# Expert weights of the last mixture loaded two units ahead into four buffers, and the next head's source terms spread one tile earlier

## What is computed

```python
scores = x @ router_w.T + router_b                  # x = layernorm of the running rows, 625 x 768
w, ids = two largest of softmax(scores), normalised # 2 of 8 experts for each row
y_e    = x @ expert_w[e].T + expert_b[e]            # expert_w[e]: 768 x 768, float32
out    = sum over the two chosen e of w_e * y_e
```

## Time and profile before

| | |
|---|---|
| median of 3 runs | 3059.64 us (3055.92 to 3059.67) |
| the profiled execution | 3062.38 us |
| its span, first to last instruction | 3060.6 us |
| busy: PE, DVE, ACT, POOL | 2528.6, 2157.8, 1362.9, 759.1 us |
| chain that ended last | PE 59%, DVE 19%, DMA 7%, POOL 6%, issue 5%, ACT 4% |
| moved by DMA | 351.82 MB, 115 GB/s in the mean |
| mean granted TensorE clock | 0.905 of full speed |
| pass 2 of the attention | about 2070 to 2180 us |
| passes 5 and 6 | about 2600 to 2665 and 2717 to 2780 us |
| units of the last mixture | about 2844 to 3028 us |

### The profile page before, as it was taken

How to read it: one execution, slowest core, us unless ns; L and a number is a source line. 1 busy time by engine, 2 the same in 40 slices (tenths; PEclk the granted TensorE clock), 3 DMA queues, 4 the chain that set the end, 5 groups by cost and what they waited for, 6 DMA issues and landing times.

```text
span 3060.6 us, 41464 instructions
## 1 busy us (share of the span) xinstructions
PE 2528.6 (83%) x12635; PEld 2024.1 (66%) x12636; DVE 2157.8 (71%) x4356; ACT 1362.9 (45%) x2651; POOL 759.1 (25%) x939
## 2 busy tenths in 40 slices
PE   5979999876999955689999999777987798888574
PEld 2536666575699934678999999736744454766573
DVE  7988888886576646788878788657764336675454
ACT  0026666562377721566656566407411100633452
POOL 4858888800066622000000000100000000001002
PEclk8979999987999985899999999888998899987797
DMA  9701100062033411777656666520000201001786
GB/s 316 246 23 34 34 31 30 21 169 84 21 45 55 40 22 35 252 254 253 226 186 218 227 224 228 172 115 1 30 31 17 67 0 47 17 1 47 269 302 210
DMA packets 83611, 351.82 MB, mean 115 GB/s; under 512 B 26984, under 2 KB 27421, under 8 KB 75950
## 3 DMA queue, kind: packets, MB, share of 16 engines
q1 hardware_dynamic: 56772, 300.70, 30.9%
q0 software_dynamic: 26656, 48.90, 5.0%
HBM read 292.28 MB, written 57.23 MB: 114 GB/s over the span
## 4 chain that ended last, share of the span: by engine, by line
PE 59%; DVE 19%; DMA 7%; POOL 6%; issue 5%; ACT 4%; SPq 0%; POOLq 0%; ACTq 0%; DVEq 0%
PE PS L853 14%; PE PS L943 10%; PE PS L990 7%; PE PS L1087 6%; PE PS L1089 3%; DMA C<-in_L_ffn_expert_w 3%; POOL logits L731 2%; PE PS L976 2%; PE PS L1106 2%; PE PS L1108 2%; PE PS L1107 2%; DVE w1s L2226 1%; DVE w3s L2319 1%; PE PS L1177 1%; DVE w2s L2231 1%
## 5 line engine op out<-in xcount | busy, mean ns | idle before, releaser
L853 PE MATMUL PS<-large_rows,turned 125*128 x1448 | 528.1, 367 | 39.5 <-issue 18.3
L853 PE MATMUL PS<-small_rows,turned 125*128 x1448 | 492.1, 343 | 0.0
L731 POOL DMA_INDIRECT logits<-lgr,key x362 | 361.8, 1000 | 248.4 <-DVE lgr L1833 175.7
L943 PE MATMUL PS<-WB,XT 128*125 128x384 f32 (+1 forms) x1120 | 389.6, 508 | 0.0
L1087 PE MATMUL PS<-urowsT,w1s 128*128 128x384 f32 (+2 forms) x1164 | 356.3, 371 | 31.5 <-DVE F L2239 19.8
L853 PEld LDWEIGHTS PS<-large_rows,turned 125*128 125x128 f32 x1448 | 272.7, 188 | 89.0 <-issue 76.7
L943 PEld LDWEIGHTS PS<-WB,XT 128*125 128x125 f32 x1120 | 213.1, 193 | 160.9 <-issue 36.3
L990 PE MATMUL PS<-F,PT 125*125 125x96 f32 (+3 forms) x1500 | 288.1, 344 | 19.2 <-ACT PT L1415 8.2
L1089 PE MATMUL PS<-urowsT,w1s 128*128 128x192 f32 (+2 forms) x1164 | 298.6, 257 | 0.0
L853 PEld LDWEIGHTS PS<-small_rows,turned 125*128 125x128 f32 x1448 | 272.3, 188 | 8.1
L990 PEld LDWEIGHTS PS<-F,PT 125*125 125x125 f32 x1500 | 226.7, 199 | 60.9 <-issue 17.9
(11 more groups left out here) (367 smaller groups left out, 5210.9 us busy)
## 6 DMA issues: line engine op xcount, KB each, us to landing
XN<-in_L_ffn_w SPq DMA_DIRECT2D x98, 769.0 KB, 4.4
PB<-in_L_ffn_w SPq DMA_DIRECT2D x97, 768.0 KB, 5.6
WB<-node_ids SPq DMA_DIRECT2D x44, 512.0 KB
C<-in_L_ffn_expert_w SPq DMA_DIRECT2D x17, 1152.0 KB, 5.4
NEG<-in_L_ffn_expert_w SPq DMA_DIRECT2D x17, 1152.0 KB, 5.4
logits<-NEG SPq DMA_DIRECT2D x8, 1367.2 KB
WB<-logits SPq DMA_DIRECT2D x5, 2187.5 KB
slot_rows<-NEG POOLq DMA_DIRECT2D x13, 768.0 KB, 56.5
```

What stands on the lines that cost most here:

```text
L731: pool.indirect_dma_start(out=table, out_offset=bass.IndirectOffsetOnAxis(ap=key[:, i:i + 1], axis=0), in_=lgr[:, i % EU, 0:HEADS[g]["h"]] ...
L853: mm = pe.matmul(out, ohT[i % 3][:, (1 - side) * P:(2 - side) * P], part[side][:, bass.ds(c, 1), a:b].rearrange("p o n -> p (o n)"), start ...
L943: mm = pe.matmul(PS[0:R, 4 + g % 4, 0:hw], XT[:, k, t * R:(t + 1) * R], w[:, k, half * hw:(half + 1) * hw], start=(k == 0), stop=(k == kc ...
```

## The change

In the last mixture the raw weights get four buffers: C, NEG, the first 2304 columns of the transposed rows XT, and of the rows XN. Unit u uses the pair u % 2. SP loads weights(1) right behind rows(0), without waiting for a split, and in the loop rows(u + 1) and then weights(u + 2); a half of unit u + 2 waits for the split of the same half of unit u. The second pair's completion semaphores are the two that counted the logit tiles earlier (they stand at 96 then). In the attention passes of kind "gat" PE's broadcast of the next head moves from in front of the turn of tile T - 2 to that of tile T - 3.

```diff
-        uw3 = [C[...][:, 0:G3], NEG[...][:, 0:G3]]
+        uw3 = [C[...][:, 0:G3], NEG[...][:, 0:G3],
+               XTz[:, 0:G3], XN[:, :, :].rearrange("p t d -> p (t d)")[:, 0:G3]]
...
-        s_m3w = [sem(f"square_expert_weights{u}") for u in range(2)]
+        s_m3w = [sem(f"square_expert_weights{u}") for u in range(2)] + s_lt
...
                 for half in range(2):
-                    wait(sp, s_l3, 2 * u + half - 1)
-                    sp.dma_start(uw3[half], ins["L3_ffn_expert_w"][bass.ds(expert, 1)]
-                                 ...[:, half * G3:(half + 1) * G3]).then_inc(s_m3w[half], 16)
+                    wait(sp, s_l3, 2 * u + half - 3)
+                    sp.dma_start(uw3[2 * (u % 2) + half], ins["L3_ffn_expert_w"][bass.ds(expert, 1)]
+                                 ...[:, half * G3:(half + 1) * G3]).then_inc(s_m3w[2 * (u % 2) + half], 16)
...
             square_rows(0)
+            square_weights(1)
             for u in range(NS):
                 if u + 1 < NS:
                     square_rows(u + 1)
-                    square_weights(u + 1)
+                if u + 2 < NS:
+                    square_weights(u + 2)
...
                 for s in range(units):
-                    if kind == "gat" and place(s)[1] == T - 2 and place(s)[0] + 1 < h:
+                    if kind == "gat" and place(s)[1] == T - 3 and place(s)[0] + 1 < h:
                         broadcast(place(s)[0] + 1)
...
-                    act.wait_ge(s_m3w[half], 16 * (u + 1))
-                    act.copy(w3s[:, 2 * (u % 2) + half, 0, :], uw3[half]).then_inc(s_h3, 1)
+                    act.wait_ge(s_m3w[2 * (u % 2) + half], 96 * (u % 2) + 16 * (u // 2 + 1))
+                    act.copy(w3s[:, 2 * (u % 2) + half, 0, :], uw3[2 * (u % 2) + half]).then_inc(s_h3, 1)
...
-                        dve.tensor_tensor(w3s[:, 2 * (u % 2) + half, 1, :], uw3[half],
+                        dve.tensor_tensor(w3s[:, 2 * (u % 2) + half, 1, :], uw3[2 * (u % 2) + half],
```

More of the change, by code:

```diff
@@ L286, in build @@
         uexp3, uexpf3, iota3 = idx[:, 0:NS], idf[:, 0, 0:NS], idf[:, 1, 0:2 * (NU + 1)]
-        uw3 = [C[:, :, :].rearrange("p t n -> p (t n)")[:, 0:G3], NEG[:, :, :].rearrange("p t n -> p (t n)")[:, 0:G3]]
+        uw3 = [C[:, :, :].rearrange("p t n -> p (t n)")[:, 0:G3], NEG[:, :, :].rearrange("p t n -> p (t n)")[:, 0:G3],
+               XTz[:, 0:G3], XN[:, :, :].rearrange("p t d -> p (t d)")[:, 0:G3]]
         bit_q = [WB[0:R, 1536 + HB * t:1536 + HB * (t + 1)].bitcast(BF16) for t in range(T)]
@@ L376, in build @@
         s_alt = [sem(f"second_edge_logits_scattered{k}") for k in range(SLOTS)]
-        s_lt = [sem(f"logit_tile_loaded{u}") for u in range(2)]
+        s_lt = [sem(f"logit_tile_loaded_then_square_weights{u}") for u in range(2)]
         s_att = sem("attention_terms_ready")
@@ L669, in square_weights @@
                 for half in range(2):
-                    wait(sp, s_l3, 2 * u + half - 1)
-                    sp.dma_start(uw3[half], ins["L3_ffn_expert_w"][bass.ds(expert, 1)]
-                                 .rearrange("o p n -> p (o n)")[:, half * G3:(half + 1) * G3]).then_inc(s_m3w[half], 16)
+                    wait(sp, s_l3, 2 * u + half - 3)
+                    sp.dma_start(uw3[2 * (u % 2) + half], ins["L3_ffn_expert_w"][bass.ds(expert, 1)]
+                                 .rearrange("o p n -> p (o n)")[:, half * G3:(half + 1) * G3]).then_inc(s_m3w[2 * (u % 2) + half], 16)
             sp.wait_ge(s_plan, 4)
```

## The result

The changed kernel took **2979.63 us** (median of 4 runs, 2978.00 to 2981.74) beside 3059.65 us before: a ratio of 0.9738, 95% interval 0.9721 to 0.9755, or 80 us less. 3000.0 were forecast with a range from 2984 to 3019, so the sign was right and the gain was larger than the range allows. The profiled execution took 2978.18 us with a span of 2976.4, 84.2 us under the span before; 4.2 us of that is where the two profiled executions stand to their medians.

What follows compares the result with a forecast made beforehand. The last mixture was taken as bound by its load, round and split latency, the attention passes by waits around the broadcast. 3062.4 - 35 - 24.7 = 3002.7, set to 3000.0 us for the runs' lower median; range 2984 to 3019.

Steps and rivals of the forecast that it cites:

- Part 1, the loop: Last mixture: latency loop of 10.38 us a unit; four weight buffers make it DMA-bound at 8.4, gain 35 us.
- I take 375: Last mixture: assumed DMA rate in GB/s with full engines, between 363 and 396, giving 8.4 us a unit.
- the prediction's own 49.5 MB: Last mixture: what DMA moves until the last weight half has landed, 132 us at 375 GB/s.
- a PE bound of 7.6 us: Last mixture: PE's time a unit, two halves of 3.37 us and 0.82 for the turning; gain 48 us at most.
- What was called untouched: Behind the last half's landing: round, split, rest of the rows, 36 products of 8.12 us and gather stay the same.
- Part 2, pass 2: Attention pass 2: broadcast one tile earlier takes 2.1 us off ACT's wait at 7 head changes, 14.7 us.
- Passes 5 and 6: Attention passes 5 and 6: the earlier broadcast removes PE's 1.67 us of idling 6 times, 10.0 us.
- Full engines move no more than the steady row says: Mixture rival: 363 GB/s or less, gain 21 to 30 us, time 3005 to 3014; chance 0.22.
- The broadcast pays half: Attention rival: ACT's own pace or DVE also holds, part 2 gives some 12 us, time 3013; chance 0.10.
- The deeper loading isn't deeper: Mixture rival: waits for rows in SP's order hold the weights back, only part 2 counts, 3035 us; chance 0.03.
- DMA nearly as fast as PE: Mixture rival: 396 GB/s and the clock's 3 us as well, time 2990; chance 0.12.
- The slow rival's chain of row loads: Mixture rival: each row load waits for the one before, 15.1 us a unit, kernel slower at 3110; chance 0.03.

Runs made afterwards that it cites:

- the runs without the depth: The changed kernel with its four buffers, but each half of the weights loaded no earlier than in the kernel before: 3024.83 us, ratio 0.9901.

## Why the prediction was wrong

- **Part 1, the loop.** That latency bound the mixture, that loading further ahead removes it, and that DMA binds next with PE close behind: right, shown by the runs without the depth, with 24 products and with fewer stores. Issues of the same buffer were expected 16.8 us apart and were 15.07, the DMA share 1.01, row landings 7.4 (about 8 was said), half landings 10 (12 was said).
- **The term that failed is the rate.** "I take 375" came from dividing the rate by the share: 305 / 0.84 = 363 and 384 / 0.97 = 396. With full queues it was 422. At 422 GB/s the prediction's own 49.5 MB take 117.3 us and not 132, so 35 us become 49.7. The last half landed 46.8 us earlier (counted from rows(0)), where 34.9 were forecast; with 1.6 us behind it that makes the 48.4 measured. The 2.9 us between 49.7 and 46.8 are a slower beginning than reckoned: from 2808.9 to 2931.4 us the mean was 408 GB/s. The highest rate that I allowed, 396, and a PE bound of 7.6 us closed the range from below. That bound added the timeline's durations, which overlap: in the earlier trace rows the products behind a turning start 0.57 us after it and not 0.82. A unit took 6.91 us where PE bound it.
- **Why the division misleads.** The share isn't a measure of how much more could be moved: at 298, 361 and 422 GB/s it was 0.80, 0.97 and 1.01. From three to four halves the rate grew by 17% and the share by 4%. The packets for one MB took 43 us of engine time with two and with three halves outstanding and 38 with four (share times 16 engines times the stretch, by the MB moved in it). So a share of 0.97 left more room than its 3%, and a full share is no fixed rate either: from 4 to 40 us the kernel before shows 1.02 at 350 GB/s, with other transfers. Why packets get shorter when more is queued isn't shown.
- By the rule of the Trainium skill (DMA: Bandwidth & Descriptors, Where 436 GB/s comes from) that some 358 GB/s bind a core's transfers with HBM a unit would have taken 8.8 us, an estimate from its figure. The runs show 422 GB/s and 7.5 us on a core whose neighbour is idle, near the 425 that the same place names as measured; the page's note above it (Measured) says that this was a single core with the other one idle.
- **What was called untouched** gave 1.6 us: the last unit's 36 products took 6.56 us and not 8.12, at a granted clock of 1.00 and not 0.79.
- **Part 2, pass 2:** 14.7 forecast, 15.2 measured, of which ACT's wait gave 14.1. What remains of the wait is 0.9 us a change (6.1 / 7), 0.8 was reckoned.
- **Passes 5 and 6:** 10.0 forecast, 13.9 measured. The idling went as worked out (5.3 a pass with hand-overs, 5.0 forecast); the 1.6 us of each pass at the lower clock, which I had put into the upper bound alone, went too, in every trace with the broadcast at T - 3. And the products of the router's stage gained 3.1 us by the clock, which I hadn't seen at all.
- The sum of the forecast's terms at their measured sizes: 48.4 + 15.2 + 13.9 + 2.8 = 80.3 us, against 80.0 between the medians; that they agree so closely is in part luck, for the router's stage alone varies by 4 us between traces. Of the 20 us that the forecast fell short, 13.4 are the mixture's (11.9 up to the last landing, by the rate, and 1.6 behind it, by the clock), 7.2 the clock's and small change in the other stages.
- **The rivals.** "Full engines move no more than the steady row says" (0.22) fell with the 422 GB/s, "The broadcast pays half" (0.10) with the 15.2 and 13.9 us, "The deeper loading isn't deeper" (0.03) with the 7.54 us a unit. "DMA nearly as fast as PE" (0.12, 2990) came nearest and was still 10 us off, for it held 396 to be the end. The slow rival's chain of row loads isn't there: without that wait nothing changes, at three halves or at four.

## What to carry to other kernels

Transfers that wait in a loop for an engine gain until the queues are full, and how full they can get isn't read from rate divided by share: take the rate from a stretch in which more is queued than the engines can move, or leave the range open upwards to it. Work out the loop with the landing time that the deeper queue will give, not the idle one: two, three and four outstanding halves gave 10.4, 8.5 and 7.5 us a unit. A hand-written order may hold a whole engine by one short operation; moving it forward pays up to the step at which its input is ready, and a step beyond that gave back here some 20 us of the 29 that the first brought.

## What the runs showed of the hardware that I had not expected

The DMA engines moved 422 GB/s over 90 us, where a quarter of the bytes were 384 KB row loads and stores and the rest halves of 1152 KB, and the landing of a half went from 5.3 to about 8 and 10 us with two, three and four outstanding. The busy share was nearly full long before the rate was (0.97 at 361 GB/s, 1.01 at 422). TensorE's clock: with the broadcast moved, PE's 1.67 us of idling at each head change of passes 5 and 6 went, and so did the fall of the granted clock to 0.50 behind the first head change of each (in pass 5 it made one sum 3.42 us long and not 1.79). In the stage behind pass 6, which the change doesn't touch, the clock fell after the turning and not within it, and 3.1 us were saved (30 transposes in 3.53 us instead of 5.08, at 1.00 all through). That the earlier broadcast brings this is shown by the kernels with and without it; that it does so through the idling is the likely reading, and no run changed the idling alone.
